# A first setup joined to its maximum, a first cross attention with a deeper column order, and the second attention's setup placed inside that cross attention's columns

## The reference

```
layer 0: performer attention (16 heads of 64; one maximum over all key features) with an ELU feed-forward,
         cross attention with ctx, ternary feed-forward
layer 1: attention over the batch axis (16 heads of 8, relative position bias, gate),
         cross attention with ctx, mixture of 64 experts
```

```
kf = exp(data_dash - diag - max(data_dash)) + eps
```

```
Sim = x w1 + ctx w2 + (x*w3) ctx^T + b_sim ;  A = softmax(Sim) ;  hq = A ctx
hc  = softmax(rowmax Sim)^T x ;  y = x + [x, hq, x*hq, x*hc] W_qv + b_qv ;  x2 = layernorm(y)
q8  = clip(round(x2 * 127/absmax)) ;  y2 = x2 + (q8 @ ternary) * step + bias ;  x3 = layernorm(y2)
```

## Time and profile before

| | us |
|---|---|
| time before, median of 3 runs | 3888.11 |
| lowest and highest of them | 3886.36, 3895.16 |
| the profiled execution's own time | 3876.06 |
| its span in the profile | 3874.2 |
| PE busy (share of the span) | 3391.5 (88%) |
| DVE, ACT, POOL busy | 2991.6, 2401.0, 1889.9 |
| setup of layer 0 up to the first product of the maximum | 0 to 39.76 |
| first cross attention, first transfer to the phase's end | 1230.69 to 1511.7 |
| second attention's setup | 1511.7 to 1546.61 |

### The profile page before, as it was taken

The page is one execution under the profiler, slowest core; times in us unless marked ns, Lnnn a source line. Parts: engine busy times, 40 slices in busy tenths (PEclk is TensorE's granted clock), DMA queues, the critical chain, the costliest instruction groups (busy, mean ns, idle before and its releaser), DMA issues. The chain is left out here.

```text
span 3874.2 us, 92251 instructions
## 1 busy us (share of the span) xinstructions
PE 3391.5 (88%) x30917; PEld 2192.8 (57%) x30917; DVE 2991.6 (77%) x6170; ACT 2401.0 (62%) x5410; POOL 1889.9 (49%) x2387
## 2 busy tenths in 40 slices
PE   6899999999685883799999977888789999999998
PEld 3466666666454782566666656777534444444443
DVE  6777777777584663798999957888868888888887
ACT  1355555556683442698999966766546565656565
POOL 1000000000473663677777743333268888888887
PEclk9999999999897876798999979898799999999999
DMA  2000000000122222000000012222176666666663
GB/s 85 7 10 9 11 9 9 11 9 10 52 60 70 58 61 39 19 17 18 18 18 18 16 29 61 72 75 73 49 152 145 141 144 141 144 140 144 141 144 85
DMA packets 285207, 243.72 MB, mean 63 GB/s; under 512 B 58472, under 2 KB 212236, under 8 KB 285068
## 3 DMA queue, kind: packets, MB, share of 16 engines
q1 hardware_dynamic: 273676, 237.22, 25.5%
q10 hardware_dynamic: 11392, 4.79, 0.5%
HBM read 210.34 MB, written 31.59 MB: 62 GB/s over the span
## 5 line engine op out<-in xcount | busy, mean ns | idle before, releaser
L2660 POOL TENSOR_TENSOR d_hidden<-d_gated,d_upper 128x512 f32<-128x512 f32 x528 | 812.5, 1564 | 177.7 <-DVE d_upper L2781 89.0
L2788 DVE TENSOR_TENSOR d_h_low<-d_hidden,d_h_high 128x512 f16<-128x512 f32 x528 | 543.9, 1030 | 120.4 <-ACT d_h_high L2736 118.6
L2730 ACT ACTIVATE d_gated<-d_g 128x512 f32<-128x512 f32 x528 | 314.6, 596 | 395.0 <-PE d_u L2676 395.0
L750 POOL MEMSET f_minus_half<- 128x4 f32 x1 | 0.1, 101 | 864.5 <-POOLq L37 864.5
L2781 DVE TENSOR_TENSOR d_upper<-d_u,d_coef 128x512 f32<-128x512 f32 x512 | 348.5, 681 | 33.1 <-DMA d_coef<-coefT 19.3
L1825 ACT ACTIVATE c_sc<-c_sc,c_negmax 128x129 f32<-128x129 f32 x1024 | 326.3, 394 | 9.2 <-issue 4.2
L2736 ACT ACTIVATE d_h_high<-d_hidden 128x512 f16<-128x512 f32 x528 | 328.3, 622 | 5.0 <-POOL d_hidden L2660 5.0
L1653 POOL TENSOR_TENSOR c_posg<-w_pos,c_gate 128x512 f32<-128x512 f32 x256 | 265.9, 1039 | 0.0
L1732 PE MATMUL c_turned<-all_ident,c_sc 128*128 128x128 f32 x1024 | 184.1, 307 | 33.7 <-ACT c_sc L1825 33.3
L2674 PE MATMUL d_g<-d_x_high,w_W_high 128*128 128x512 f16 x528 | 200.6, 380 | 11.2 <-POOL d_x_low L2653 8.2
L2674 PE MATMUL d_o<-d_h_high,w_W_high 128*128 128x512 f16 x528 | 200.1, 379 | 2.1 <-ACT d_h_high L2736 1.7
(11 more groups left out here) (407 smaller groups left out, 9685.6 us busy)
## 6 DMA issues: line engine op xcount, KB each, us to landing
d_coef<-coefT SPq DMA_DIRECT2D x256, 512.0 KB, 7.1
d_cT<-in_ctxT SPq DMA_DIRECT2D x128, 64.0 KB, 2.0
d_stage<-in_moe_W SPq DMA_DIRECT2D x48, 128.0 KB, 2.1
mx_x<-in_xT SPq DMA_DIRECT2D x16, 256.0 KB
b_x<-in_x SPq DMA_DIRECT2D x64, 64.0 KB
y<-b_y SPq DMA_DIRECT2D x64, 64.0 KB, 1.6
f_y<-y SPq DMA_DIRECT2D x16, 256.0 KB, 3.4
f_x<-in_x SPq DMA_DIRECT2D x16, 256.0 KB, 3.6
```

The costliest lines, as they stand in the source:

```text
L2660: nc.gpsimd.tensor_tensor(hidden[b][:], gated[b][:], upper[b][:], ALU.mult).then_inc(h_ready, 1)
L2730: nc.scalar.activation(gated[b][:], ps_g[i][:], ACT.Silu, scale=1.0 / W_SCALE).then_inc(silu_ready, 1)
L2788: nc.vector.tensor_tensor(h_low[b][:], hidden[b][:], h_high[b][:], ALU.subtract).then_inc(h_low_ready, 1)
```

## The change

1. **First setup.** `setup_l0` is taken apart: `weights_l0` and `whole_l0` only allocate, and the work goes into `phase_max`. SP loads WkT, projT, the first x, WqT, the second x, and then the 13 others; PE fuses the keys first, then the queries; only Wkp is split ahead of the products, the other four behind the x groups on ACT and POOL. The tiles of the maximum become 128 x 1024 (4 of them, each two banks, one reduction each).
2. **Cross attention.** Columns run from -2 to 21. `norm1` goes from -1 to -2, `norm2` from -4 to -5, `scales`, `round8`, `turn_q8`, `copy_q8`, `ternary`, `bias_x2` and `steps` from -2 to -3, `add_ffn` and the second `power` from -3 to -4, the store from -4 to -6; `copy_means`, `by_hq` and `by_hc` come into the group's own column; the second statistics are a part of their own. All lists are reordered.
3. **Second setup.** `Stage1` holds the tensors; its steps are put in columns of `phase_cross0`; the table is turned by ACT alone, two copies in each of columns 9 to 16, and its reads are all SP's.

The core of the diff of `phase_max` (SP, ACT, PE):

```
+                sp.dma_start(whole["WkT"][:], d["WkT"][:]).then_inc(keys_loaded, 16)
+                for half in (slice(0, 64), slice(64, 128)):
+                    sp.dma_start(whole["projT2"][half, :], d["projT"][:]).then_inc(keys_loaded, 16)
+                load_x(0, 0)
+                sp.dma_start(whole["WqT"][:], d["WqT"][:]).then_inc(queries_loaded, 16)
+                load_x(0, 1)
+                for dst, src in rest:
+                    sp.dma_start(dst[:], src[:]).then_inc(rest_loaded, 16)
...
+                for j in range(U):
+                    high(0, j)
+                act.wait_ge(joined, 1)
+                out, of = halves("Wkp", 1)
+                nc.scalar.activation(out, of, ACT.Copy, scale=DN).then_inc(other_scaled, 1)
+                act.wait_ge(other_scaled, 1)
+                act.wait_ge(half_scaled, 1)
+                nc.scalar.activation(w["Wkp"][0][:], whole["Wkp"][:], ACT.Copy, scale=L0_SCALE["Wkp"]).then_inc(key_high, 1)
+                act.wait_ge(joined, 2)
+                for hh in range(2):
...
+                for n, k in enumerate(SPLIT):
+                    nc.scalar.activation(whole[k][:], whole[k][:], ACT.Copy, scale=L0_SCALE[k]).then_inc(scaled, 1)
+                    act.wait_ge(scaled, n + 1)
+                    nc.scalar.activation(w[k][0][:], whole[k][:], ACT.Copy).then_inc(split_high, 1)
...
+                def products(it, j):
+                    pe.wait_ge(low_ready, U * it + j + 1)
+                    for i in range(WIDE):
+                        if not (is_first(it) and j == 0):
+                            pe.wait_ge(part_ready, WIDE * (U * it + j - 1) + i + 1)
+                        elif i == 3:
+                            pe.wait_ge(query_scaled, 2)
+                        for a in range(2):
+                            last = thrice(nc, dd[i][:, GROUP * a:GROUP * (a + 1)], [p[:, 2 * i + a, :] for p in w["Wkp"]], [p[:, group(it, j)] for p in xT_parts])
+                        last.then_inc(dd_ready, 1)
...
+                pe.wait_ge(keys_loaded, 16 * 3)
+                join("WkT", "Wkp")
+                pe.wait_ge(queries_loaded, 16)
+                join("WqT", "Wqp")
+                pe.wait_ge(key_low, 1)
+                for j in range(U):
+                    products(0, j)
```

```
-            for c in range(-2, GROUPS + 4):
+            for c in range(-2, GROUPS + 6):
                 def at(shift, part, *more, c=c):
...
-                def column(at):
+                def column(at, c):
                     at(2, load)
-                    at(-4, store)
+                    at(-6, store)
+                    if c == -1:
+                        sp.dma_start(t.onehot[:], t.d["onehot"][:]).then_inc(t.first_loaded, 16)
+                        sp.dma_start(t.rel[:], t.d["rel_emb"][:]).then_inc(t.first_loaded, 16)
+                        sp.dma_start(t.w["next_b"][:], t.d["qvk_b"][:, 1:3, :].to_broadcast([P, 2, D])).then_inc(t.rows_loaded, 16)
+                    if c == 0:
+                        for dst, src in t.loads:
+                            sp.dma_start(dst[:], src[:]).then_inc(t.loaded, 16)
+                    if c == 2:
+                        sp.wait_ge(t.biases_ready, 1)
+                        sp.dma_start(t.skew.ap().rearrange("t h k -> h t k"), t.biases[:].unsqueeze(1).to_broadcast([H, 8, t.SPAN])).then_inc(t.skewed, 16)
+                    if 3 <= c < 7:
+                        sp.wait_ge(t.skewed, 16)
+                        for h in range(4 * (c - 3), 4 * (c - 3) + 4):
+                            sp.dma_start(t.pos_flat[8 * h:8 * h + 8, :, H:H + B + 1], t.shifted(h, 0, B + 1)).then_inc(t.pos_loaded, 16)
+                            sp.dma_start(t.pos_flat[8 * h:8 * h + 8, :, 0:H], t.shifted(h, B - H, H)).then_inc(t.pos_loaded, 16)
+                    if c == 7:
+                        sp.wait_ge(t.cleared, 1)
+                        for slot in range(3):
+                            for a in range(4):
+                                at_row = 32 * a + D // H * slot
+                                sp.dma_start(t.grep_w[at_row:at_row + D // H, :], t.d["grep_w"][:]).then_inc(t.loaded, 16)
+                        sp.wait_ge(t.rows_loaded, 16)
+                        for part, k in enumerate(("bias_v", "bias_k")):
...
-                def column(at):
-                    at(-1, by_hq)
-                    at(-1, by_hc)
+                def column(at, c):
+                    at(0, normalise)
+                    at(-3, bias_x2)
+                    at(-3, steps)
+                    at(-4, power, 1, x3_ready)
+                    at(0, by_hq)
+                    at(0, by_hc)
+                    at(-1, power, 0, x2_ready)
                     at(0, bias_x)
-                    at(0, normalise)
-                    at(-3, power, 1, x3_ready)
-                    at(-2, bias_x2)
-                    at(-2, steps)
-                    at(-1, power, 0, x2_ready)
...
+                    if g == 0:
+                        pe.wait_ge(t.biases_ready, 1)
                     for i in range(N):
                         last = nc.tensor.matmul(tile(quant, i), tile(q8T[g % 2], i), w["ternT"][:], start=True, stop=True)
...
-                def column(at):
+                def column(at, c):
                     at(0, similarities)
                     at(1, turn_x)
                     at(-1, features)
                     at(0, turn_peaks)
-                    at(-2, turn_q8)
+                    at(-3, turn_q8)
                     at(0, turn_e)
-                    at(-2, ternary)
+                    at(-3, ternary)
                     at(0, attend)
                     at(0, turn_weights)
                     at(0, means)
+                    if c == 0:
+                        pe.wait_ge(t.relb_ready, 1)
+                        nc.tensor.matmul(quant[0:H, 0:t.SPAN], t.relb[:], t.onehot[:], start=True, stop=True).then_inc(t.spread, 1)
                 by_column(column)
...
-                def column(at):
-                    at(-4, norm2)
+                def column(at, c):
                     at(0, exps)
                     at(1, copy_x)
+                    at(-2, norm1)
+                    at(-3, copy_q8)
                     at(0, row_exps)
-                    at(-2, copy_q8)
                     at(0, copy_e)
+                    at(-5, norm2)
                     at(0, copy_hq)
-                    at(-1, norm1)
+                    if 9 <= c < 17:
+                        act.wait_ge(t.pos_loaded, 16 * 2 * H)
+                        for g in range(2 * (c - 9), 2 * (c - 9) + 2):
+                            nc.scalar.activation(*t.turned(g), ACT.Copy)
...
                     last.then_inc(y2_ready, 1)
+                def stats2(g):
                     dve.wait_ge(y2_ready, g + 1)
                     dve.sem_inc(waited, 1)
...
-                def column(at):
-                    at(-1, copy_means)
-                    at(-2, scales)
+                def gate_setup():
+                    w1, own = t.w, Own(dve, t.own)
...
+                def column(at, c):
                     at(0, peaks)
-                    at(-2, round8)
+                    at(-3, scales)
                     at(0, totals)
-                    at(-3, add_ffn)
+                    at(-3, round8)
+                    at(-4, add_ffn)
+                    at(0, row_tops)
+                    at(-4, stats2)
+                    at(0, row_weights)
                     at(-1, add_x)
-                    at(0, row_tops)
+                    at(0, copy_weights)
                     at(-1, stats1)
-                    at(0, row_weights)
-                    at(0, copy_weights)
+                    at(0, copy_means)
+                    if c == 0:
+                        dve.wait_ge(t.first_loaded, 16 * 2)
+                        nc.vector.tensor_scalar(t.relb[:], t.rel[:], -1.0, None, ALU.mult).then_inc(t.relb_ready, 1)
+                    if c == 1:
+                        dve.wait_ge(t.spread, 1)
+                        nc.vector.tensor_copy(t.biases[:], quant[0:H, 0:t.SPAN]).then_inc(t.biases_ready, 1)
+                    if c == GROUPS + 2:
+                        gate_setup()
                 by_column(column)
```

More of the change, by code:

```diff
@@ L239, in setup_l0, with whole_l0 @@
-    return w
+    return w
+def whole_l0(t):
+    DH, PAIRS = 64, H // 2
+    whole = {k: t.sb(k, [P, PAIRS, P]) for k in PROJECTED}
+    whole.update({k: t.sb(k, [P, PAIRS, D]) for k in ("WqT", "WkT")})
+    whole.update(projT2=t.sb("projT2", [P, DH]), b2_rows=t.sb("b2_rows", [2, D]), low_row=t.sb("low_row", [2, 1]))
+    return whole
 def setup_cross0(nc, ph, d, ident):
@@ new lines, in _ @@
+                for hh in range(2):
+                    out, of = halves("Wqp", hh)
+                    nc.scalar.activation(out, of, ACT.Copy, scale=DN).then_inc(query_scaled, 1)
+                with nc.scalar.Fori(1, steps) as it:
+                    for j in range(U):
```

(48 more changed lines are left out.)

299 lines of the change are left out of this document (104 added, 195 removed).

## The result

The changed kernel takes 3782.9 us (median of 4 runs, 3777.5 to 3792.0) against 3890.9 for the kernel before beside it (4 runs, 3886.4 to 3895.2): ratio 0.9725, 95% interval 0.9702 to 0.9748, 108 us by the medians. On another chip (experiment e9) the ratio was 0.9713 (0.9696 to 0.9731). The forecast was 3798, with 3778 to 3830 as its range.

A forecast was written before the change was run, and what follows sets the result against it. It took transfer waits to bound both setups and a 14.8 us loop through DVE, POOL and ACT to bound the cross attention columns. Savings 25.4 + 26.5 + 4 + 34 = 89.9; 3888.1 - 89.9 = 3798 us, range 3778 to 3830.

The forecast's parts named there:

- The first setup: Start of the kernel: reordered loads bring the first product from 39.8 to 14.3 us, saving 25.4, bounds 22 and 28.
- The columns: Cross attention: first interval 14.3 us, the other 14 at 13.2, 199.1 against 225.6; 26.5 saved, bounds 4 and 42.
- VectorE's list down to `copy_weights`: Cross attention column: VectorE's part of the remaining chain after the score maxima, put at 9.4 us.
- stretch of `round8`: Cross attention column: `round8` on VectorE now runs beside GpSimd's `normalise`; between 0 and 1.47 us added, 0.6 taken.
- clock: Cross attention column: PE's narrow products at half clock cost 2.0 us; 0.9 from the mean clock 0.77, 0.5 taken.
- the rival of the full lock: Cross attention: `round8` and `normalise` exclude each other in every column, 0.9 us more in 14 columns; 3810, chance 0.13.
- the floor of 12.1: Cross attention: columns of 12.1 us if clock stays up and the lock costs nothing; as rival 3781, chance 0.20.
- the loop: Cross attention: once per column through DVE, POOL, ACT, DVE, 14.8 us; `norm1` one column later removes 5.5.
- the columns don't shorten: Cross attention: rival that another loop of about 14.8 us takes over, PE at half clock above all; 3825, chance 0.15.
- Drain and second setup: End of cross attention saves 4 us (bounds 0 and 6); the second attention's setup, moved into columns, saves 34.0.
- the 1.4: First of the 15 column intervals: the bias rows' product on PE with its hand-over adds 1.4 us.
- The strict sequence: Whole kernel: phases stand in strict sequence, so each touched stretch was judged by what ends last in it.

The follow-up runs named there:

- e9: The changed kernel run again unaltered, on another chip; ratio 0.9713 to the kernel before, columns 186.5 us.
- e8: Kernel before with the joined first setup alone and 112 more ScalarE instructions (waits already met) ahead of the final loop; ratio 0.9931 to the kernel before.
- e3: Kernel before with the joined first setup and the cross attention steps in new columns, lists in old order; ratio 0.9948, columns 207.8 us.
- e10: Kernel before with the joined first setup and new list order, each step in its old column; ratio 1.0019, columns 232.7 us.
- e11: Kernel before with the joined first setup and new step columns, only VectorE's list in new order; ratio 1.0022, columns 232.7 us.
- e2: Kernel before with the new first setup and all column changes, second setup still its own phase; ratio 0.9900, columns 184.1 us.
- e1: Kernel before with the joined first setup alone; ratio 0.9996, final phase 1077.3 us.
- e7: Kernel before with 2 more ScalarE instructions (waits already met) in the final phase's first group; ratio 1.0062, final phase 1082.2 us.
- e5: Changed kernel with 8 more ScalarE instructions (waits already met) in the final phase's first group; ratio 0.9774 to the kernel before.
- e12: Changed kernel with four more GpSimd multiplications behind `normalise`, into a tile nobody reads; ratio 0.9718 to the kernel before, columns 186.1 us.

## Why the prediction was right, and where it was off

**The first setup, 25.4 forecast.** Measured 25.2 in the stages, and 27 (19 to 35) in e8. The order WkT, projT, x, WqT, x and the chain behind it came as worked out. The splits moved under the maximum were covered: from the first product to the next phase are 89.4 us, where I had left 88.0.

**The columns, 26.5 forecast; 36.5 (39.2 in e9) measured.** This is the term that was mis-sized. The first column came as forecast (14.41, forecast 14.3); the other fourteen took 12.48 and, in e9, 12.29, where the sum had 13.2. The column shown above can be held against the sum term by term; the rightmost figures are means of the last eleven columns of e9, read from the timeline in the same way.

| us | forecast | column at 1322.86 | last eleven of e9 |
|---|---|---|---|
| VectorE's list down to `copy_weights`, without stretch | 9.4 | 8.25 | 8.36 |
| stretch of `round8` and the rounding behind it | 0.6 | 0.92 | 1.10 |
| TensorE to the next score maxima, and hand-overs | 2.7 | 2.67 | 2.70 |
| clock | 0.5 | in the line above | in the line above |
| column | 13.2 | 11.84 | 12.16 |

- VectorE's list is the step that failed most: 9.4 was put together from rows of the kernel before, in which two operations ran beside GpSimd. `b_wide`, 0.74 in the earlier trace rows, takes 0.28 in every column now; one operation of `scales` (L1259, then L1363) took some 0.37 in most columns and takes 0.17. The new order ended these overlaps, which gives some 0.7, and made the one of `round8`.
- The exclusion was put too low, not too high. The Trainium skill, SBUF — State Buffer, "Who interferes with whom", states that a VectorE operation in a 2-port mode and a GpSimd operation exclude each other for a whole instruction. The trace agrees in that `round8` is stretched (279 to 514 and 526 ns), by 0.9 to 1.1 us a column of the 1.47 that the rival of the full lock would add. That rival's time (3810) missed because the list under it is shorter; its mechanism is nearer to the trace than the 0.6. That this stretch is time of the column is read from the trace, in which VectorE has no wait to absorb it; no experiment shows it.
- The clock. I argued from the mean of before; with PE's waits gone the clock was 0.87 to 0.89 in the columns, `similarities` ran at 1.03 in the column shown, and next to nothing of the 0.5 is left.

So 9.4 and 0.5 were too high and 0.6 too low. That the floor of 12.1 is so near the 12.2 to 12.5 measured is in part luck, since it had no stretch in it.

How `norm1` is taken out of the loop was right in mechanism and too simple. Distance alone gives 18 of 41.6 us (e3), the order of the lists alone loses 7 (e10), VectorE's order with the distance loses 7 too (e11), and all of it gives 41.6 (e2). I had argued VectorE's list only; the gain needs those of GpSimd, PE and ScalarE as well. That the columns don't shorten (3825) was a real case: it is e10 and e11.

**Drain and second setup, 4 and 34.0 forecast, 38.5 measured together.** Right, also apart: in e2, with the setup still a phase, the stretch from the last score maxima to the second attention's first load is 77.8, so the drain gave 3.1 of the 80.9 and the setup 35.4. That the setup in the columns is free apart from the first was off by 0.6 to 3.6 us beyond the 1.4: e2, without it, has 184.1, and the changed kernel 186.1 to 189.1.

**The sum.** 25.2 + 36.5 + 38.5 = 100.2 against 89.9: 3888.1 - 100.2 = 3788. The 5 us to the 3783 measured are within the scatter of single executions: the unchanged second attention took 744 to 754 us in these profiles, with no tie to what was changed.

**The strict sequence**, by which a shorter phase moves all that follows forward by as much, held for this kernel by luck, not by its argument. In e1 it did not: some 20 us were given back 2,700 us later, by a few instructions more on ScalarE (4 by the trace; in e7, 2 were enough). The changed kernel has six fewer there than the kernel before; 8 more make it stall (e5). Had parts 1 and 2 come without part 3, as in e2, the prediction's own sum for them (56) would have been 13 to 17 above the 39 to 43 measured, and nothing in it would have said why.

## What to carry to other kernels

Where a kernel has hardware loops, a change in one phase moves the code of all later ones. Compare the stages that weren't touched and the packets of the instruction queues first, before a gain that doesn't show is explained in the stage that was changed. Where an operation is stretched beside another engine, look whether its engine has a wait in the same column that could absorb the stretch, and see that an experiment takes the overlap away and does not only move it. And when steps are put into an order by hand, distance and order of all engines are one edit: each half here was worth less than half, or cost time.

## What the runs showed of the hardware that was not expected

- A loop body of 351 ScalarE instructions stalled the engine 3.8 to 6.2 us at each jump back, or not at all, depending on where it stood: 2 more instructions ahead of it gave the kernel before five stalls (e7: 25.7 us, 25 more packets of the instruction queue), and 112 more took the five of e1 away (e8). PE's clock fell to its lower level behind a stall: in e1, after PE had stood 3.26 us, matmuls of 0.38 us took 0.63 at 3081. The final phase took 1069 to 1082 us with the stalls and 1055 to 1060 without.
- The place in the built program gave the edge only to within a few instructions (2384 good in one kernel, 2382 stalled in another). The count of executed ScalarE instructions in the traces put it between 6421 and 6423, in line with every run.
- Beside GpSimd, some of VectorE's operations are stretched and others are not: the four of `round8` averaged 514 to 526 ns against 279 before, `b_wide` took 0.74 us against 0.28, and the four of `add_ffn` stayed at 336 ns with four more GpSimd operations beside them (e12).
